# The first two feed-forward tiles multiplied in turn by quarters, with a third result buffer

## The reference

```python
def reference(x, w_qkv, w_proj, kernel, bias):       # x: (1, 8192, 2048)
    x = x + attention(layernorm(x), w_qkv, w_proj)   # 16 heads of 128
    return x + ffn(layernorm(x), kernel, bias)

def ffn(x, kernel, bias):                            # kernel: (2048, 2048)
    bq = fake_quant(bias, 8, -1)
    xq = fake_quant(x, 8, -1)                        # a scale per token
    kq = fake_quant(kernel, 8, 0)                    # a scale per output column
    y = relu(einsum('bsd,df->bsf', xq, kq) + bq)
    return fake_quant(y, 8, -1)                      # a scale per token
```

## Time and profile before

| what | us |
|---|---|
| median of 3 runs | 643.17 (642.28 to 647.33) |
| the profiled execution | 647.92 |
| its span on the slowest core, core 5 | 646.4 |
| spans of the eight cores | 633.5 to 646.4 |

### The profile page before, as it was taken

How to read it: one execution, slowest core, us unless ns; L and a number is a source line. 1 busy time by engine, 2 the same in 40 slices (tenths; PEclk the granted TensorE clock), 3 DMA queues, 4 the chain that set the end, 5 groups by cost and what they waited for, 6 DMA issues and landing times.

```text
span 646.4 us, 9466 instructions; the slowest of 8 cores (633.5 to 646.4 us)
## 1 busy us (share of the span) xinstructions
PE 608.7 (94%) x3416; PEld 302.7 (47%) x3416; DVE 316.8 (49%) x492; ACT 239.4 (37%) x492; POOL 41.0 (6%) x80
## 2 busy tenths in 40 slices
PE   5789999999999999999999999999979979999993
PEld 5645444444444444444444555554544424444442
DVE  3853445435354340010012456867748635778657
ACT  3862123221331320100002667675647323453331
POOL 0100100000000011111100000000000000000000
PEclk8899999999999999999999999999989999999997
DMA  8998789999999999999834989999999992332313
GB/s 243 268 202 209 158 207 231 199 255 221 228 227 222 248 175 163 165 151 157 119 61 60 184 143 244 199 179 196 147 251 207 260 321 60 98 97 106 122 66 130
DMA packets 88974, 116.02 MB, mean 179 GB/s; under 512 B 69089, under 2 KB 69089, under 8 KB 85217
## 3 DMA queue, kind: packets, MB, share of 16 engines
q1 hardware_dynamic: 77986, 75.58, 46.2%
q0 software_dynamic: 10944, 39.85, 37.5%
HBM read 109.12 MB, written 23.08 MB: 205 GB/s over the span
## 4 chain that ended last, share of the span: by engine, by line
PE 67%; SPq 23%; DMA 6%; DVE 2%; issue 1%; ACT 1%; DVEq 0%; ACTq 0%; POOLq 0%
PE pF L804 49%; PE pF L909 16%; SPq L263 11%; SPq L253 4%; SPq L240 3%; SPq L272 3%; DMA wqb<-wqkv 2%; DMA xbuf<-x_att 2%; DMA kq<-kq_spill 2%; DVE cols L536 1%; SPq L247 1%; PE pF L928 1%; PE pF L822 1%; ACT aT L403 0%; ACT abuf L397 0%
## 5 line engine op out<-in xcount | busy, mean ns | idle before, releaser
L804 PE MATMUL pF<-aT,wqb 128*128 128x512 bf16 x1504 | 327.1, 379 | 2.0 <-DMA wqb<-wqkv 2.0
L804 PEld LDWEIGHTS pF<-aT,wqb 128*128 128x128 bf16 x1504 | 146.5, 98 | 176.2 <-issue 2.3
L886 PE MATMUL pF<-wpq,qT 128*128 128x512 bf16 x512 | 120.9, 382 | 0.0
L909 PE MATMUL pF<-kq,xqT 128*128 128x512 bf16 x496 | 108.8, 382 | 4.8 <-DMA kq<-kq_spill 3.6
L909 PEld LDWEIGHTS pF<-kq,xqT 128*128 128x128 bf16 x496 | 48.6, 98 | 65.1 <-issue 7.9
L886 PEld LDWEIGHTS pF<-wpq,qT 128*128 128x128 bf16 x512 | 48.1, 99 | 48.1 <-issue 1.6
L428 ACT ACTIVATE Ebuf<-pF,cols 128x128 bf16<-128x128 f32 x128 | 45.6, 369 | 40.7 <-DVE cols L598 39.6
L560 DVE CAST vT<-pF 128x512 bf16<-128x512 f32 x16 | 11.0, 690 | 80.8 <-PE pF L804 80.8
L354 POOL DMA_DIRECT2D wqb<-wqkv x48 | 26.0, 541 | 295.5 <-PE pF L804 244.3
L560 DVE CAST kT<-pF 128x512 bf16<-128x512 f32 x16 | 11.1, 692 | 63.0 <-PE pF L804 63.0
L661 DVE SCALAR_TENSOR_TENSOR tt<-pF,cols,bqb 128x512 f32<-128x512 f32 x31 | 23.2, 750 | 38.1 <-PE pF L909 37.9
(11 more groups left out here) (69 smaller groups left out, 485.3 us busy)
## 6 DMA issues: line engine op xcount, KB each, us to landing
wqb<-wqkv POOLq DMA_DIRECT2D x48, 512.0 KB, 8.6
wkf<-wkT SPq DMA_DIRECT2D x16, 1024.0 KB, 7.6
xbuf<-x_att SPq DMA_DIRECT2D x8, 1024.0 KB, 16.5
kr_spill<-kqr SPq DMA_DIRECT2D x16, 512.0 KB, 11.3
wpq<-wp POOLq DMA_DIRECT2D x16, 512.0 KB, 9.6
xr<-x_res SPq DMA_DIRECT2D x8, 1024.0 KB, 8.3
out<-xr SPq DMA_DIRECT2D x7, 1024.0 KB, 4.2
kq_spill<-kst POOLq DMA_DIRECT2D x12, 512.0 KB, 8.8
```

Of the source, the lines that this page charges most:

```text
L804: mm = tn.matmul(pF[QBANK[j]][:, :], wqb[e % NW][:, 128 * c:128 * (c + 1)], aT[:, 8192 * h + 512 * c: 8192 * h + 512 * (c + 1)], start=(c ...
L886: mm = tn.matmul(pF[SLOTB[f % 3]][:, :], sT[:, 2048 * b + 128 * m: 2048 * b + 128 * (m + 1)], wpq[u][:, 512 * m:512 * (m + 1)], start=(m = ...
L909: mm = tn.matmul(pF[y % 4][:, :], xqT[:, 2048 * k + 128 * c: 2048 * k + 128 * (c + 1)], w[:, c, :, :], start=(c == 0), stop=(c == NC - 1))
```

## The change

The first eight quarters of the feed-forward product are no longer done tile by tile (four quarters of tile 0, four of tile 1) but in turn: quarter 0 of tiles 0 and 1, quarter 1 of tiles 0 and 1, and so on. From tile 2 on the order is as before. The list `YORD` gives the order, `YIDX` the place of each pair in it, and the PSUM bank and the counted waits follow the place. Results of tiles go to three buffers in place of two; the third lies where the fifth `kst` buffer, `Ebuf` and `aTT` were. `y_round(0)` moves from slot Y0+5 to Y0+8 and `y_add(0)` from Y0+7 to Y0+10; `y_round(1)` and `y_add(1)` keep their slots, Y0+9 and Y0+11. The order written out for SyncE isn't changed. What the diff below leaves out is the replacement of `tt[k % 2]` by `tt[k % 3]` in `y_round`, `y_scale`, `y_add` and the code of the last tile, and the same new order in the counted waits.

```diff
@@ -36,6 +36,10 @@
 NS = Y0 + 32
+
+YORD = ([(k, u) for u in range(4) for k in range(2)]
+        + [(k, u) for k in range(2, NT) for u in range(4)])
+YIDX = {ku: y for y, ku in enumerate(YORD)}
@@ -112,8 +116,8 @@
-    tt = [A(f"tt{i}", [128, 2048], F32, offset=180224 + 8192 * i)
-          for i in range(2)]
+    tt = [A(f"tt{i}", [128, 2048], F32,
+            offset=180224 + 8192 * i if i < 2 else 200704) for i in range(3)]
...
@@ -515,16 +519,18 @@
                 r = sl - Y0 - 5
-                if r >= 0 and r % 4 == 0 and r // 4 < NT - 1:
+                if r in (3, 4):
+                    y_round(r - 3)
+                if r >= 8 and r % 4 == 0 and r // 4 < NT - 1:
                     y_round(r // 4)
@@ -652,26 +658,27 @@
             def y_evac(k, u):
-                v.wait_ge(S_("yMM"), 4 * k + u + 1)
+                y = YIDX[(k, u)]
+                v.wait_ge(S_("yMM"), y + 1)
...
                 return inc(v.scalar_tensor_tensor(
-                    tt[k % 2][:, cs], pF[(4 * k + u) % 4][:, :], cc(C_SX[k]),
+                    tt[k % 3][:, cs], pF[y % 4][:, :], cc(C_SX[k]),
                     bqb[:, cs], ALU.mult, ALU.add), "yEv")
...
@@ -718,7 +725,7 @@
                 if Y0 <= f < NS - 1:
-                    k, u = (f - Y0) // 4, (f - Y0) % 4
+                    k, u = YORD[f - Y0]
@@ -744,7 +751,9 @@
                 r = sl - Y0 - 7
-                if r >= 0 and r % 4 == 0 and r // 4 < NT - 2:
+                if r in (3, 4):
+                    y_add(r - 3)
+                if r >= 8 and r % 4 == 0 and r // 4 < NT - 2:
                     y_add(r // 4)
@@ -892,7 +901,7 @@
             def y_part(k, u, c0, c1):
-                y = 4 * k + u
+                y = YIDX[(k, u)]
@@ -966,7 +975,7 @@
                     elif sl < NS - 1:
-                        y_part((sl - Y0) // 4, (sl - Y0) % 4, c0, c1)
+                        y_part(*YORD[sl - Y0], c0, c1)
```

More of the change, by code:

```diff
@@ L467, in y_round @@
                 s.wait_ge(S_("yS"), k + 1)
-                h = inc(s.activation(tt[k % 2][:, :], tt[k % 2][:, :], AF.Copy,
+                h = inc(s.activation(tt[k % 3][:, :], tt[k % 3][:, :], AF.Copy,
                                      bias=MAGIC, scale=cc(C_RY[k])), "sS")
                 wt(s, h)
-                inc(s.activation(tt[k % 2][:, :], tt[k % 2][:, :], AF.Relu,
+                inc(s.activation(tt[k % 3][:, :], tt[k % 3][:, :], AF.Relu,
                                  bias=cc(C_NMG)), "yZ")
@@ L523, in _ @@
                 cs = slice(512 * u, 512 * (u + 1))
-                h = inc(s.activation(tt[k % 2][:, cs], tt[k % 2][:, cs], AF.Copy,
+                h = inc(s.activation(tt[k % 3][:, cs], tt[k % 3][:, cs], AF.Copy,
                                      bias=MAGIC, scale=cc(C_RY[k])), "sS")
                 wt(s, h)
-                inc(s.activation(tt[k % 2][:, cs], tt[k % 2][:, cs], AF.Relu,
+                inc(s.activation(tt[k % 3][:, cs], tt[k % 3][:, cs], AF.Relu,
                                  bias=cc(C_NMG)), "yQ")
@@ L666, in y_scale @@
                 wt(v, h)
-                h = inc(v.reduce_max(cc(C_YM[k % 2]), tt[k % 2][:, :], AX.X),
+                h = inc(v.reduce_max(cc(C_YM[k % 2]), tt[k % 3][:, :], AX.X),
                         "vS")
@@ L673, in y_add @@
                 v.wait_ge(S_("yZ"), k + 1)
-                inc(v.scalar_tensor_tensor(xr_tile(k), halves(tt[k % 2]),
+                inc(v.scalar_tensor_tensor(xr_tile(k), halves(tt[k % 3]),
                                            cc(C_SY[k]), xr_tile(k), ALU.mult,
@@ L728, in _ @@
                             h_y0 = inc(v.reduce_max(
-                                cc(C_YM[k % 2] + 1), tt[k % 2][:, 0:1024], AX.X),
+                                cc(C_YM[k % 2] + 1), tt[k % 3][:, 0:1024], AX.X),
                                 "vS")
@@ L733, in _ @@
                             h_y1 = inc(v.reduce_max(
-                                cc(C_YM[k % 2] + 2), tt[k % 2][:, 1024:1536],
+                                cc(C_YM[k % 2] + 2), tt[k % 3][:, 1024:1536],
                                 AX.X), "vS")
@@ L755, in _ @@
                 h_ev = inc(v.scalar_tensor_tensor(
-                    tt[k % 2][:, cs], pF[3 + h2][:, 0:256], cc(C_SX[k]),
+                    tt[k % 3][:, cs], pF[3 + h2][:, 0:256], cc(C_SX[k]),
                     bqb[:, cs], ALU.mult, ALU.add), "yEv")
@@ L759, in _ @@
                 h_y2 = inc(v.reduce_max(cc(C_YM[k % 2] + 3 + h2),
-                                        tt[k % 2][:, cs], AX.X), "vS")
+                                        tt[k % 3][:, cs], AX.X), "vS")
             wt(v, h_y2)
@@ L767, in _ @@
                 cs = slice(512 * u, 512 * (u + 1))
-                tu = tt[k % 2][:, cs]
+                tu = tt[k % 3][:, cs]
                 if u >= 2:
```

## The result

The changed kernel took 641.22 us as the median of 14 runs, the kernel before 646.96, also in 14. Some executions of either kernel run slower than the rest, with a mean granted clock of down to 0.81 on the cores of one die; the ratio of 0.989, with a 95% interval of 0.9856 to 0.9925, leaves them out, and with them the profiled execution of 645.85 us. So the change makes the kernel some 1.1% faster, between 0.75% and 1.44%.

The account below looks back on a forecast made before the run. A late load of kq[2], and behind it TensorE, was taken to bound core 5, the slowest. The wait of 3.63 plus 1.52 for the clock gave 5.15 us, taking 643.17 to 638.0 us; range 634.0 to 641.8.

Parts of the forecast that it names:

- What bounds: Feed-forward stage, core 5: the late load of kq[2], held in SyncE's queue, sets the end; a 3.63 us TensorE wait.
- The new order: First eight feed-forward quarters: the 3.63 us wait on core 5 goes; on core 0 a wait of 1.3 us stays.
- The clock: Third quarter on core 5, slow after idle time: 1.52 us counted back, bounds 0 and 1.52.
- VectorE, ScalarE, SyncE, the third buffer, each costed at 0: Side effects in the feed-forward stage: VectorE lags of 1.9 and 2 to 3 us, held transpose, moved rounding; cost 0.
- The cover of 10.4 us: Feed-forward stage: four banks let VectorE lag three quarters, 10.4 us, before TensorE waits.
- The sum: Whole kernel: 5.15 us saved on core 5, profiled execution 647.92 to 642.8, median 643.17 to 638.0, 0.8% less.
- the first rival: Slowest core: core 5's late entry is an accident of that execution; 6.4 to 9.5 us gained; chance 0.30.
- the first of the three signs: Ahead of the feed-forward stage: prediction wrong if the slowest core enters later than before for reasons of earlier stages.
- Slower by VectorE: Feed-forward stage: VectorE's lag makes TensorE wait; slower only beyond 15.6 us of lag, 17 would give 644.6; chance 0.02.
- Slower by the clock: Feed-forward stage: a stream without gaps lowers the granted clock; 0.10 lower would give about 649; chance 0.03.
- the limiter named beside it: Trainium skill's limiter: 13/16 of the clock once three of a die's cores run dense matmuls; stage estimated at 132 us.
- the change does nothing: Third quarter's wait: if it were for transposed tile 1 rather than weights, nothing would move, 643.2; chance 0.03.

Follow-up runs that it names:

- The last experiment: The changed kernel with the stage's first quarter waiting only for its own bank's evacuation, the second for the last one; ratio 0.991 to the kernel before.

## Why the prediction was right

**What bounds.** The reading that the late load of quarter 2 sets the end, and SyncE's queue makes it late, held. Issued earlier, the wait on it nearly goes; with the order of quarters changed it goes altogether. What the prediction left out is that quarter 3 was late too: before, four of the eight cores waited 1.4 to 1.8 us for it ahead of the fourth quarter, and on core 7 that was the whole wait. The new order moves its first need by three places as well, so nothing came of the omission.

**The new order.** Forecast: no wait on core 5, 3.3 us to spare for quarter 2. The stage is 107.05 us on all cores against the 107.2 worked out. A wait of 1.3 us was forecast for a core like core 0 of the profile before, whose load was issued 3.9 us behind the start of the stage and took 11.2 us; no core of this execution nor of the one with two buffers shows a wait, but none had its load issued later than 2.3 us behind the start, so that case wasn't met. The last experiment came closest: on its core 1 the load was issued 3.65 us behind the start and landed 9.8 us later, without a wait. The swap of the loads shows that it was a real possibility: there, waits of up to 3.4 us come from quarter 2 taking some 14 to 17 us to land.

**The clock.** The 1.52 us counted back were right as far as the mechanism goes: filled, the gap doesn't slow the third quarter; the same fall comes behind a wait for VectorE. The size is that of core 5: on cores 0 and 4 before, the stage lost 3.0 us beyond its waits. That filling alone didn't shorten the stage wasn't foreseen, and it says that the 1.52 us could be had only together with the later need of quarter 3.

**VectorE, ScalarE, SyncE, the third buffer, each costed at 0.** The lags of 1.9 and 2 to 3 us came out as 1.8 and 2.9, and the transpose of tile 5 held nobody. The cover of 10.4 us stood: three more maxima cost nothing, six cost 5.35 us of waiting where some 6 were expected. The buffer alone moves nothing, and it can be left out if tile 0's addition comes two slots earlier.

**The sum.** The forecast was 0.8% less; measured are 1.1%, with 0.8% just inside the interval. 1.1% of 643 are 7.1 us, more than the 5.15 of core 5, and inside the band of the first rival (6.4 to 9.5 us gained); the interval, 4.8 to 9.3 us, reaches into both. The medians of the 14 runs each are 5.7 us apart; the forecast's 638.0 was counted from the 643.17 of three runs and isn't comparable as it stands. The mechanism is the forecast's, which the stage on every core shows. The weak term is the choice of core 5 as the one that counts. In the runs on record the slowest core is now one, now another, with either kernel, so that core 5 was last in the profile was an accident, as the first rival had it. That its loss, 5.3 us, is close to the mean of the eight cores, 5.7 us, is luck: they range from 2.0 on core 7 to 11.0 on core 0. Whether the slowest core gains more than the mean one, which would explain 1.1% rather than 0.8%, the interval is too wide to tell.

The sum for the profiled execution, 642.8, failed: it took 645.85. Its slowest core, core 0, entered the stage at 523.49, core 5 before at 520.31. So 5.3 us were won in the stage and 3.2 lost ahead of it, which is the first of the three signs that the prediction named for being wrong. The later entry isn't the work of the change as far as the runs show: in the kernel before with the gap filled, a core enters at 525.27, and the mean entry of the eight cores is 514.1 in the kernel before, 515.3 in the changed one, and 516.2 with the third buffer alone in the old order.

**The rivals.** Slower by VectorE needed 15.6 us of lag; the lag was 2.9. Slower by the clock: in the profiled execution the granted clock stays at 1.00 in the stage on all eight cores with no gap left, so neither the rival nor the limiter named beside it found a case there. That is said of this execution alone. That the change does nothing is excluded.

## What to carry to other kernels

When a load comes late, ask first what else could be computed with what is already there: two tiles of rows on the same weight quarter double the time until the next quarter is wanted, at no cost in matmuls, and in the stage that was worth more than moving the load forward in its queue (5.7 us against 3.4), where the loads then took longer to land. Cost such a reordering by the number of steps by which each engine's buffer covers the new lumps of work, here three quarters of 3.46 us (a lag of 10.2 us cost nothing, one of 15.7 cost 5.35), and check the margin of each load against its landing time. An idle stretch on TensorE costs more than its length when the clock falls behind it, so a gap of 3.6 us was worth 5.1; but filling the gap with idle work returns nothing where another load is next.

## Not expected

Loads issued earlier landed more slowly: the last of the three loads took 18.0 us from issue to landing when all three were issued within 6.7 us ahead of the transpose, against 14.2 behind it. Over the eight cores the slowest of the three took 16.8 us in the mean against 14.6 in the kernel before.

Short waits don't all cost the clock: on core 0 of the kernel before the fall came with 7.54 us of idle time, on core 1 of the filled kernel with 2.06, while behind the 1.82 us of the kernel before's core 7 the stage ran on at full speed, with 172 matmuls in 37.28 us. Nor does length alone decide it: the 3.08 us above didn't bring the fall, 2.06 and 2.08 did. What else does wasn't tried.

The cores enter the stage at very different times, 510.3 to 523.5 us in one execution of the changed kernel, though they run the same program; since the stage is now equal on all, this spread is the whole spread of the spans, 631.1 to 644.3. The execution of the last experiment has the same spread, 510.3 to 524.5. What makes a core late ahead of the stage wasn't tried here and stays open.
